# Multiplying the second table's rows by the second layer's weights in layer 1 instead of layer 2 (graph convolution and experts kernel)

## The chip, the cores and the metric

The kernel runs on one core of a Trainium2 chip. The metric is the device time of one execution in microseconds (us), the median over several executions. A difference of 0.2% is about what the measurement of this kernel can tell from none.

## What is computed

There are N = 12500 nodes with D = 256 features and E = 200000 weighted edges. The input is layer-normalised, goes through two graph convolutions, is added to the input, layer-normalised again and sent through a mixture of 8 experts of which each row uses 2.

```python
def _gcn_conv(x, src, dst, ew, W, b, n_nodes):
    xW = x @ W
    deg = segment_sum(ew, dst) + 1.0
    dinv = rsqrt(deg)
    norm = dinv[src] * ew * dinv[dst]
    agg = segment_sum(norm[:, None] * xW[src], dst)
    agg = agg + (dinv * dinv)[:, None] * xW
    return agg + b

h1 = relu(_gcn_conv(layernorm(x), ..., W1, b1))
h2 = relu(_gcn_conv(h1, ..., W2, b2))
x = x + h2
t = layernorm(x)
out = x + t + sum_e combine[:, e] * (gelu(t @ w1[e] + b1[e]) @ w2[e] + b2[e])
```

Everything is float32. The sum over edges is linear, so the product with a layer's weights can be taken before the sum or after it.

## The kernel before

**Setup (to about 234 us).** Edges are sorted by destination. They are cut into 392 groups of 512 edges (4 tiles of 128). Degrees and statistics are worked out, and a first table `ytab[0]` is stored in HBM: normalised rows of x times `dinv`, 98 blocks of 128 nodes. The same rows, transposed, start the accumulator `accbuf` (features on partitions, nodes along the free axis).

**A layer.** GpSimd (POOL) walks through the 392 groups, and for each it issues four indirect DMAs (L480) that gather 128 rows each of the table into `msg`, a ring of MR = 5 groups. Before it writes a ring place again it waits for `s_part`, the count of groups that TensorE has finished. VectorE builds for each tile a one-hot selection times the edge weight (`selection`, L1105). TensorE multiplies (`products`, L811): 8 matmuls per group, a [feature, node] sum over a window of 96 nodes. VectorE adds it into `accbuf` (`add`, L1113). In layer 1 the first group of each pair waits for the messages of both groups.

**A slot.** After every 4 groups one block of 128 nodes is finished; there are 98 such slots in a layer.

In layer 1 a slot is: ScalarE copies the block's sums to `aggS` (`sums`, L562); TensorE multiplies them by the weights (`sums`, L747: two matmuls of 128x256 into `psG`); VectorE scales and adds the bias (`linear`, L1162), then takes the maximum with 0 and scales by `dinv` (`table2`, L1169) into `yS`, which is the row block of the second table; SyncE stores it to `ytab[1]` (L400); TensorE transposes it (`turn_y2`, L755, two transposes) and ScalarE copies the result back into `accbuf` (`back`, L567) as the start of layer 2's sums. Layer 2's gathers may begin only when all 98 blocks are stored (`s_y2out`).

In layer 2 the slot starts alike (`sums` with `gw[1]`, L747, then `linear`), adds the input row, normalises (`moments`, `newton`, `token`), transposes the token (`turn_tok`, L764), computes the router's logits (L772) and the combine weights, and runs the 8 experts: `hidden` (L796), Gelu on ScalarE (L593), `project` (L805) and `share` on VectorE (L1233). Every engine's order is written out by hand. TensorE spreads the experts of the slot before (`last`) between the four groups of the current slot; `sums(1, s)` stands between `hidden(last, 2)` and `project(last, 1)`.

A float32 matmul is two records in the trace, a transpose is one; so `sums` shows as x4, `turn_y2` as x2 and a group of `products` as x16.

Of the kernel before, what the change touches and what calls it, by code (L numbers as in the profile page):

```python
# [8 lines left out]
ALU = mybir.AluOpType  # L9
# [11 lines left out]
R = 4  # L21
# [33 lines left out]
def build(nc, x, src, dst, ew, gw1, gb1, gw2, gb2, rw, ew1, eb1, ew2, eb2, out):  # L55
# [123 lines left out]
    yS = xS  # L179
    res = [sb(f"res{u}", [P, D]) for u in range(2)]  # L180
# [32 lines left out]
    ps_lin, ps_b2 = psG[:, 0:D], psG[:, D:2 * D]  # L213
    ps_tok, ps_lg, ps_comb = psT[:, 0:D], psT[:, D:D + NEXP], psT[0:NEXP, 384:512]
# [69 lines left out]
    s_linD = [sem(f"s_linD{l}") for l in range(2)]  # L284
    s_y2 = sem("s_y2")
# [208 lines left out]
    def _(act):  # L494
# [62 lines left out]
        def sums(l, s):  # L557
            wait(act, s_lin[l], s.k - 1)
            if l == 0:
                wait(act, s_y2C, s.k - 1)  # L560
            stand(act, s)
            act.activation(aggS[:, :, :], accT[:, :, bass.ds(s.col, P)], ACT.Copy).then_inc(s_agg[l], 1)  # L562

        def back(s):
            act.wait_ge(s_y2T, s.k)
            stand(act, s)
            act.activation(accT[:, :, bass.ds(s.col, P)], ps_tok.rearrange("p (k n) -> p k n", k=KD), ACT.Copy).then_inc(s_y2C, 1)  # L567
# [28 lines left out]
        def late0(s):  # L596
            sums(0, s)
            back(s)
# [10 lines left out]
        for k in range(1, NI + 1):  # L609
            s = Slot(k, k % 2, col=slot_word(act, C1, k))  # L610
            act.wait_ge(s_added, k * R)
            sums(0, s)
            back(s)
# [28 lines left out]
    def _(pe):  # L642
# [97 lines left out]
        def sums(l, s, biases_behind=1):  # L740
            pe.wait_ge(s_agg[l], s.k)
            wait(pe, s_linD[l], s.k - 1)
            if l == 1:
# [4 lines left out]
            m.then_inc(s_lin[l], 1)  # L748

        def turn_y2(s):  # L750
            pe.wait_ge(s_y2, s.k)
            wait(pe, s_y2C, s.k - 1)
            stand(pe, s)
            for k in range(KD):
                t = pe.transpose(psT[:, k * P:(k + 1) * P], yS[s.u][:, k * P:(k + 1) * P], ident[:, :])  # L755
            t.then_inc(s_y2T, 1)
# [83 lines left out]
        def late0(s):  # L840
            sums(0, s)
            turn_y2(s)
# [13 lines left out]
        for i in range(NI):  # L856
            s = Slot(i, i % 2) if i else None
            group(0, R * i)
            group(0, R * i + 1)
# [6 lines left out]
        sums(0, Slot(NI, NI % 2))  # L866
        turn_y2(Slot(NI, NI % 2))
# [56 lines left out]
    def _(v):  # L924
# [317 lines left out]
        def late0(s):  # L1242
            linear(0, s)
            table2(s)
# [20 lines left out]
        v.wait_ge(s_spare, 16)  # L1265
# [3 lines left out]
        for i in range(NI):  # L1269
            s = Slot(i, i % 2, entry=slot_word(v, E1, i)) if i else None  # L1270
            bases = bases_at(v, NI - 1 - i)
            for r in range(R):
                q = i * R + r
                add(q, bases[R - 1 - r])
                if q + R < NG:
                    selection(q + R)
                if s and r == 1:
                    linear(0, s)
                    table2(s)
        s = Slot(NI, NI % 2, entry=slot_word(v, E1, NI))  # L1280
        linear(0, s)
        table2(s)
# [88 lines left out]
```

## Time and profile before

| what | value |
|---|---|
| median of 3 runs | 4566.18 us (4564.49 to 4569.79) |
| the profiled execution | 4561.83 us |
| its span | 4560.0 us |
| TensorE busy over the span | 82% |
| GpSimd busy over the span | 67% |
| VectorE, ScalarE busy | 49%, 16% |
| setup, layer 1, layer 2 | to 234 us, to 2212 us, to the end |
| granted TensorE clock, 1000 to 2000 us | 0.75 |
| granted TensorE clock, 2400 to 3400 us | 1.00 |

The profile is one execution; its time is 4.35 us (0.1%) under the median. "Busy" is the union of the instructions of an engine, and TensorE's weight loads are counted apart (PEld). A line of the timeline gives start, length, engine, line and operation, how many records it merges, and in brackets the idle time ahead of it and what ended that. As matmuls overlap, the cost of a run of matmuls in a dense stretch is the distance from its start to the start of the next run, which is shorter than its own length. The granted clock of 1.00 is 2.4 GHz, 0.50 is 1.2 GHz.

### The profile page before, as it was taken

Reading aid. Unit: us, or ns where it says so; the run is one execution under the profiler, and the core shown is the slowest. Engines: PE = TensorE matmul, PEld = TensorE weight load, DVE = VectorE, ACT = ScalarE, POOL = GpSimd, SP = SyncE. Lnnn points to the kernel's source line nnn. Section 1 sums busy time; section 2 is a strip of 40 time slices with the busy share of each in tenths; the row PEclk is TensorE's granted clock in tenths of the full one; section 3 lists DMA queues with packets and bytes.
Section 4 is the critical chain, followed back from the end, with each engine's and each line's share of the span. In section 5 each row is a group of like instructions: output and inputs, shape, how many; then the busy total and the mean of one; then the engine's idle time right before and its main releaser. Section 6 shows DMA issues by size and latency. Waiting matters only on the chain.

```text
span 4560.0 us, 77688 instructions
## 1 busy us (share of the span) xinstructions
PE 3746.5 (82%) x27282; PEld 3519.0 (77%) x27283; DVE 2222.0 (49%) x8238; ACT 725.4 (16%) x2287; POOL 3035.8 (67%) x3196
## 2 busy tenths in 40 slices
PE   6756666666666666666699999999999999999999
PEld 5556565656656655665699999999999999999999
DVE  7623232332333323223366666666666666666665
ACT  1300000000000000000022222222222222222222
POOL 2177777777777777777676666666666666666663
PEclk9967777777777777777799999999999999999999
DMA  6443333333333333333333333333333333333331
GB/s 144 120 135 111 112 112 112 111 112 112 111 112 112 111 112 112 111 112 112 100 112 101 104 101 99 101 102 102 103 101 99 101 102 102 103 100 100 101 102 56
DMA packets 242001, 488.03 MB, mean 107 GB/s; under 512 B 59886, under 2 KB 140089, under 8 KB 241612
## 3 DMA queue, kind: packets, MB, share of 16 engines
q0 software_dynamic: 150528, 411.24, 31.9%
q1 hardware_dynamic: 84424, 66.74, 4.8%
q10 hardware_dynamic: 6660, 5.02, 0.4%
q8 instruction: 225, 3.69, 0.3%
q14 instruction: 164, 1.34, 0.1%
HBM read 444.10 MB, written 38.67 MB: 106 GB/s over the span
## 4 chain that ended last, share of the span: by engine, by line
PE 54%; POOL 31%; issue 11%; DMA 3%; DVE 0%; ACT 0%; SPq 0%; ACTq 0%; DVEq 0%; POOLq 0%
POOL msg L480 31%; PE part L811 16%; PE psY L805 16%; PE psH L796 15%; PE psG L747 2%; DMA msg<-ytab,srcT 1%; PE psG L787 1%; PE psT L772 1%; PE psY L687 1%; DMA ytab<-msg 1%; PE psH L811 1%; PE psT L764 0%; POOL sel L452 0%; PE psY L811 0%; PE psG L687 0%
## 5 line engine op out<-in xcount | busy, mean ns | idle before, releaser
L480 POOL DMA_INDIRECT msg<-ytab,srcT x3136 | 2987.9, 953 | 1362.4 <-issue 893.1
L811 PE MATMUL part<-sel,msg 128*128 128x96 f32 x8384 | 1147.7, 299 | 270.8 <-DMA msg<-ytab,srcT 270.8
L811 PEld LDWEIGHTS part<-sel,msg 128*128 128x128 f32 x8384 | 1121.8, 216 | 297.9 <-DMA msg<-ytab,srcT 254.4
L796 PEld LDWEIGHTS psH<-work,wbuf 128*128 128x128 f32 x6272 | 808.7, 192 | 34.8
L805 PE MATMUL psY<-wbuf,work 128*128 128x256 f32 x3136 | 829.6, 387 | 0.0
L1105 DVE TENSOR_SCALAR sel<-iota,relT,ewT 128x96 f32<-128x96 f32 x3136 | 826.4, 341 | 2.3 <-ACT accbuf L553 1.4
L796 PE MATMUL psH<-work,wbuf 128*128 128x128 f32 x6272 | 811.1, 275 | 0.0
L593 ACT ACTIVATE work<-psH,b_s 128x128 f32<-128x128 f32 x1568 | 489.7, 363 | 1586.1 <-PE psH L796 1586.1
L1113 DVE TENSOR_TENSOR accbuf<-accbuf,part 128x192 f32 x524 | 185.7, 354 | 1076.7 <-PE part L811 1076.6
L805 PEld LDWEIGHTS psY<-wbuf,work 128*128 128x128 f32 x3136 | 543.7, 191 | 77.5 <-issue 32.5
L811 PE MATMUL psY<-sel,msg 128*128 128x96 f32 x2080 | 388.6, 374 | 236.6 <-DMA msg<-ytab,srcT 236.6
L811 PEld LDWEIGHTS psY<-sel,msg 128*128 128x128 f32 x2080 | 377.6, 286 | 257.2 <-DMA msg<-ytab,srcT 257.2
L811 PE MATMUL psH<-sel,msg 128*128 128x96 f32 x2080 | 379.1, 368 | 235.4 <-DMA msg<-ytab,srcT 235.4
L811 PEld LDWEIGHTS psH<-sel,msg 128*128 128x128 f32 x2080 | 368.4, 279 | 256.0 <-DMA msg<-ytab,srcT 256.0
L1233 DVE SCALAR_TENSOR_TENSOR work<-psY,comb,work 128x256 f32<-128x256 f32 x686 | 329.3, 480 | 56.4 <-PE psY L805 35.2
L567 ACT ACTIVATE accbuf<-psT 128x256 f32 x98 | 37.5, 383 | 1849.2 <-PE psT L755 1849.2
L1113 DVE TENSOR_TENSOR accbuf<-accbuf,psY 128x192 f32 x130 | 46.1, 355 | 463.6 <-PE psY L811 463.6
L1113 DVE TENSOR_TENSOR accbuf<-accbuf,psH 128x192 f32 x130 | 46.1, 355 | 451.8 <-PE psH L811 451.8
L747 PE MATMUL psG<-gw,work 128*128 128x256 f32 x784 | 205.4, 385 | 1.1 <-ACT work L562 1.1
L1162 DVE SCALAR_TENSOR_TENSOR work<-psG,dinv,gb 128x256 f32<-128x256 f32 x196 | 94.2, 480 | 103.4 <-PE psG L747 103.4
L747 PEld LDWEIGHTS psG<-gw,work 128*128 128x128 f32 x784 | 135.2, 193 | 11.4 <-ACT work L562 1.3
L452 POOL TENSOR_TENSOR sel<-sel,ewT 128x192 f32<-128x192 f32 x49 | 44.1, 899 | 101.2 <-DVE sel L966 95.8
(184 smaller groups left out, 1768.8 us busy)
## 6 DMA issues: line engine op xcount, KB each, us to landing
msg<-ytab,srcT POOLq DMA_INDIRECT x3136
ytab<-xS SPq DMA_DIRECT2D x99, 128.0 KB, 1.9
ytab<-msg SPq DMA_DIRECT2D x98, 128.0 KB, 1.9
xS<-in_x SPq DMA_DIRECT2D x98, 128.0 KB
out<-res SPq DMA_DIRECT2D x98, 128.0 KB
accbuf<-in_x SPq DMA_DIRECT2D x97, 128.0 KB, 3.2
wbuf<-in_L_ffn_w ACTq DMA_DIRECT2D x2, 2048.0 KB, 14.8
wbuf<-in_dst SPq DMA_DIRECT2D x1, 588.0 KB
```

The source lines that it names most:

```text
L480: pool.indirect_dma_start(msg[:, r * GT + j, :], None, ytab[l], bass.IndirectOffsetOnAxis(ap=srcT[:, g * GT + j:g * GT + j + 1].bitcast(U3 ...
L593: g = act.activation(hS[:, e % 2, m, :], psH[e % 2][:, m * P:(m + 1) * P], ACT.Gelu, bias=b1_s[:, e, m:m + 1])
L687: m = pe.matmul(wbanks[t // SB][0:LO, at_col:at_col + HI], wlo[:, h, r * GT + k, :], whi[:, h, r * GT + k, :], start=(k == 0), stop=(k == ...
L747: m = pe.matmul(ps_lin, aggS[:, k, :], gw[l][:, k, :], start=(k == 0), stop=(k == KD - 1))
L772: m = pe.matmul(ps_lg, tokS[s.u][:, k, :], rwT[:, k, :], start=(k == 0), stop=(k == KD - 1))
L796: mm = pe.matmul(psH[e % 2][:, m * P:(m + 1) * P], w1_s[:, e, k, m * P:(m + 1) * P], tokS[s.u][:, k, :], start=(k == 0), stop=(k == KD - 1))
L805: mm = pe.matmul(psY[e % 2][:, 0:D], hS[:, e % 2, m, :], w2_s[:, e, m, :], start=(m == 0), stop=(m == KD - 1))
L811: m = pe.matmul(slot[:, h * W:(h + 1) * W], msg[:, tile0 + j, h * P:(h + 1) * P], sel[:, sel0 + j, :], start=(j == 0), stop=(j == GT - 1))
L1105: t = v.tensor_scalar(sel[:, r * GT + j, :], iota[:, 0:W], relT[:, g * GT + j:g * GT + j + 1], ewT[:, g * GT + j:g * GT + j + 1], ALU.is_e ...
L1113: v.tensor_tensor(to, to, sums_of(q // NG, q % NG)[:, 0:KD * W].rearrange("p (k w) -> p k w", k=KD), ALU.add).then_inc(s_added, 1)
L1162: v.scalar_tensor_tensor(lin[:, :], ps_lin, dinv[:, bass.ds(s.entry, 1)], gb[l][:, :], ALU.mult, ALU.add).then_inc(s_linD[l], 1)
L1233: v.scalar_tensor_tensor((mix if e < NEXP - 1 else res[s.u])[:, :], psY[e % 2][:, 0:D], comb[s.u][:, e:e + 1], (mix if e else front[s.u])[ ...
```

## The change

In layer 1, VectorE now writes the hidden rows to `h1` (a buffer that layer 2 uses for `tok`), not to `yS`. TensorE transposes them (`turn_h1`), ScalarE copies them to `h1T`, TensorE multiplies them by `gw[1]` (`table2`, two matmuls of 128x256 into the second half of `psG`), and ScalarE copies the product to `yS`. From there the store, the two transposes and the copy back go as before, but half a slot to a slot later. In layer 2, `sums` no longer multiplies by `gw[1]`: it turns the sums by two transposes into the same place.

```diff
@@ ScalarE
+        def hidden1(s):
+            act.wait_ge(s_h1T, s.k)
+            wait(act, s_tab, s.k - 1)
+            act.activation(h1T[:, :, :], ps_h1.rearrange("p (k n) -> p k n", k=KD), ACT.Copy).then_inc(s_h1C, 1)
+        def table2(s):
+            act.wait_ge(s_tab, s.k)
+            wait(act, s_y2out, (s.k - 2) * 16)
+            wait(act, s_y2T, s.k - 2)
+            act.activation(yS[s.u][:, :], ps_tab, ACT.Copy).then_inc(s_y2, 1)
-        def back(s):
+        def back(s, taken):
             act.wait_ge(s_y2T, s.k)
+            act.wait_ge(s_agg[0], taken)
...
-        for k in range(1, NI + 1):
-            s = Slot(k, k % 2, col=slot_word(act, C1, k))
-            act.wait_ge(s_added, k * R)
-            sums(0, s)
-            back(s)
+        for k in range(1, NI + 2):
+            last, s = s, Slot(k, k % 2, col=slot_word(act, C1, k)) if k <= NI else None
+            if last:
+                hidden1(last)
+                table2(last)
+            if s:
+                act.wait_ge(s_added, k * R)
+                sums(0, s)
+            if last:
+                back(last, min(k, NI))
@@ TensorE
             for k in range(KD):
-                m = pe.matmul(ps_lin, aggS[:, k, :], gw[l][:, k, :], start=(k == 0), stop=(k == KD - 1))
+                if l == 0:
+                    m = pe.matmul(ps_lin, aggS[:, k, :], gw[0][:, k, :], start=(k == 0), stop=(k == KD - 1))
+                else:
+                    m = pe.transpose(ps_lin[:, k * P:(k + 1) * P], aggS[:, k, :], ident[:, :])
+        def turn_h1(s):
+            pe.wait_ge(s_h1, s.k)
+            wait(pe, s_y2C, s.k - 1)
+            for k in range(KD):
+                t = pe.transpose(ps_h1[:, k * P:(k + 1) * P], h1[:, k * P:(k + 1) * P], ident[:, :])
+            t.then_inc(s_h1T, 1)
+        def table2(s):
+            pe.wait_ge(s_h1C, s.k)
+            pe.wait_ge(s_linD[0], s.k)
+            for k in range(KD):
+                m = pe.matmul(ps_tab, h1T[:, k, :], gw[1][:, k, :], start=(k == 0), stop=(k == KD - 1))
+            m.then_inc(s_tab, 1)
...
             if s:
                 sums(0, s)
-            group(0, R * i + 2)
-            group(0, R * i + 3)
-            if s:
-                turn_y2(s)
+            if last:
+                turn_y2(last)
+            if i < NI:
+                group(0, R * i + 2)
+                group(0, R * i + 3)
+            if s:
+                turn_h1(s)
+                table2(s)
@@ VectorE
-        def table2(s):
+        def hidden1(s):
             v.wait_ge(s_linD[0], s.k)
-            wait(v, s_y2out, (s.k - 2) * 16)
-            wait(v, s_y2T, s.k - 2)
+            wait(v, s_h1T, s.k - 1)
-            v.tensor_scalar(yS[s.u][:, :], lin[:, :], 0.0, dinv[:, bass.ds(s.entry, 1)], ALU.max, ALU.mult).then_inc(s_y2, 1)
+            v.tensor_scalar(h1[:, :], lin[:, :], 0.0, dinv[:, bass.ds(s.entry, 1)], ALU.max, ALU.mult).then_inc(s_h1, 1)
...
-        v.wait_ge(s_spare, 16)
```

The wait on `s_spare` (the store of the padding rows) moves from VectorE to ScalarE.

TensorE's order over one slot in the middle of layer 1, before: two groups, the sums' product, two groups, the transposes of the table's block.

```order
L811 MATMUL part<-sel,msg 128x96 [waits s_sel,s_msg3]
L811 MATMUL part<-sel,msg 128x96 x7
L747 MATMUL psG<-gw,work 128x256 [waits s_linD0,s_agg0]
L747 MATMUL psG<-gw,work 128x256
L811 MATMUL psH<-sel,msg 128x96 [waits s_sel,s_msg4,s_msg0]
...
L811 MATMUL psH<-sel,msg 128x96 x7
L755 MATMUL psT<-ident,xS 128x128 [waits s_y2C,s_y2]
L755 MATMUL psT<-ident,xS 128x128
L811 MATMUL psY<-sel,msg 128x96 [waits s_sel,s_msg1,s_msg2]
```

The same place after the change. L864 is `products`, L781 the sums' product, L808 the transposes of the table's block (now of the slot before), L792 the transposes of the hidden rows, L800 the product with `gw[1]`.

```order
L864 MATMUL part<-sel,msg 128x96 [waits s_sel,s_msg3]
L864 MATMUL part<-sel,msg 128x96 x7
L781 MATMUL psG<-gw,work 128x256 [waits s_y2,s_linD0,s_agg0]
L781 MATMUL psG<-gw,work 128x256
L808 MATMUL psT<-ident,xS 128x128 [waits s_y2C,s_y2]
L808 MATMUL psT<-ident,xS 128x128
L864 MATMUL psH<-sel,msg 128x96 [waits s_sel,s_msg4,s_msg0]
...
L864 MATMUL psH<-sel,msg 128x96 x7
L792 MATMUL psT<-ident,work 128x128 [waits s_y2C,s_h1]
L792 MATMUL psT<-ident,work 128x128
L800 MATMUL psG<-gw,work 128x256 [waits s_linD0,s_h1C]
L800 MATMUL psG<-gw,work 128x256
```

The table's transposes moved from behind the second pair to behind the sums' product, one slot later; behind the second pair stand two transposes and two matmuls with a wait for ScalarE (`s_h1C`) between them.

TensorE's order in layer 2 around `sums(1, s)`, before and then after (L805 and L858 are `project`, L796 and L849 `hidden`):

```order
L796 MATMUL psH<-work,wbuf 128x128 [waits s_gelu]
L796 MATMUL psH<-work,wbuf 128x128 x3
L747 MATMUL psG<-gw,work 128x256 [waits s_bias,s_linD1,s_agg1]
L747 MATMUL psG<-gw,work 128x256
L805 MATMUL psY<-wbuf,work 128x256 [waits s_yadd,s_gelu]
```

```order
L849 MATMUL psH<-work,wbuf 128x128 [waits s_gelu]
L849 MATMUL psH<-work,wbuf 128x128 x3
L784 MATMUL psG<-ident,work 128x128 [waits s_bias,s_linD1,s_agg1]
L784 MATMUL psG<-ident,work 128x128
L858 MATMUL psY<-wbuf,work 128x256 [waits s_yadd,s_gelu]
```

Two transposes of 128 columns stand where two matmuls of 256 columns stood, with the same waits.

## Rows read from the trace of the kernel before

**Rows 1.** The page, busy time of each engine over the span.
```profile
PE 3746.5 (82%) x27282; PEld 3519.0 (77%) x27283; DVE 2222.0 (49%) x8238; ACT 725.4 (16%) x2287; POOL 3035.8 (67%) x3196
```

**Rows 2.** Windows: stretch, length, busy us of each engine, PEclk, DMA share, GB/s.
```profile
1000.00:2000.00 1000.00, 640.27 (x3486) 605.78 (x3485) 303.14 (x1099) 39.96 (x100) 756.85 (x799) 0.75 0.39 112
2400.00:3400.00 1000.00, 1000.00 (x7332) 943.40 (x7331) 636.15 (x2458) 256.81 (x850) 650.30 (x680) 1.00 0.36 102
```

**Rows 3.** Groups by form, 600 to 2100 us (layer 1): GpSimd's gathers.
```profile
L480 POOL DMA_INDIRECT msg<-ytab,srcT x1198 | 1135.8, 948 | 364.8 <-issue 359.1 <-PE part L811 2.4 <-PE psH L811 1.8
```

**Rows 4.** Timeline of one slot of layer 1, TensorE.
```profile
1502.15 0.38 PE L755 MATMUL psT<-ident,xS 128*128 128x128 f32 x2
...
1508.55 6.54 PE L811 MATMUL part<-sel,msg 128*128 128x96 f32 x32 [6.02 <-DMA msg<-ytab,srcT]
...
1514.93 1.06 PE L747 MATMUL psG<-gw,work 128*128 128x256 f32 x4
...
1518.48 3.81 PE L811 MATMUL psH<-sel,msg 128*128 128x96 f32 x32 [2.49 <-DMA msg<-ytab,srcT]
```

**Rows 5.** Timeline of TensorE in layer 2: transposes, sums, and the last slot's sums.
```profile
3407.17 0.38 PE L764 MATMUL psT<-ident,work 128*128 128x128 f32 x2
3407.39 1.92 PE L811 MATMUL part<-sel,msg 128*128 128x96 f32 x16
...
3420.30 1.03 PE L747 MATMUL psG<-gw,work 128*128 128x256 f32 x4
3421.17 1.03 PE L805 MATMUL psY<-wbuf,work 128*128 128x256 f32 x4
...
4528.02 1.03 PE L747 MATMUL psG<-gw,work 128*128 128x256 f32 x4
```

**Rows 6.** Timeline of the other engines in the same slot of layer 2.
```profile
3420.50 0.62 ACT L593 ACTIVATE work<-psH,b_s 128x128 f32<-128x128 f32 x2 [1.49 <-PE psH L796]
...
3421.47 0.48 DVE L1162 SCALAR_TENSOR_TENSOR work<-psG,dinv,gb 128x256 f32<-128x256 f32 x1 [1.02 <-PE psG L747]
...
3426.87 0.94 POOL L480 DMA_INDIRECT msg<-ytab,srcT  x1 [2.39 <-PE part L811]
...
3430.10 0.41 DVE L1194 TENSOR_SCALAR work<-work,mv,rs 128x256 f32<-128x256 f32 x1
...
3430.66 0.25 PEld L764 LDWEIGHTS psT<-ident,work 128*128 128x128 f32 x2
```

**Rows 7.** Timeline, from layer 1's last group to layer 2's first gather.
```profile
2205.33 0.38 PE L755 MATMUL psT<-ident,xS 128*128 128x128 f32 x2
...
2205.75 0.38 ACT L567 ACTIVATE accbuf<-psT 128x256 f32 x1 [19.30 <-PE psT L755]
2206.32 0.42 ACT L562 ACTIVATE work<-accbuf 128x256 f32 x1 [0.19 <-ACT accbuf L567]
...
2206.79 1.13 PE L747 MATMUL psG<-gw,work 128*128 128x256 f32 x4 [1.08 <-ACT work L562]
2208.06 0.48 DVE L1162 SCALAR_TENSOR_TENSOR work<-psG,dinv,gb 128x256 f32<-128x256 f32 x1 [2.08 <-PE psG L747]
2208.58 0.35 DVE L1169 TENSOR_SCALAR xS<-work,dinv 128x256 f32<-128x256 f32 x1
...
2209.10 0.33 SPq L400 DMA_DIRECT2D ytab<-xS  x1
...
2211.91 0.94 POOL L480 DMA_INDIRECT msg<-ytab,srcT  x1 [13.96 <-DMA ytab<-xS]
```

**Rows 8.** Windows and timeline, start of layer 2, at the lower clock level.
```profile
2212.00:2225.00 13.00, 3.81 (x18) 3.84 (x19) 1.41 (x6) 0.00 (x0) 9.96 (x11) 0.50 0.60 114
...
2221.19 6.88 PE L811 MATMUL part<-sel,msg 128*128 128x96 f32 x32 [11.77 <-DMA msg<-ytab,srcT]
...
2241.89 1.97 PE L747 MATMUL psG<-gw,work 128*128 128x256 f32 x4
...
2243.65 2.46 PE L811 MATMUL part<-sel,msg 128*128 128x96 f32 x16
```

More of the change, by code:

```diff
@@ L179, in build @@
     yS = xS
+    h1, h1T = tok, tokS[0]
     res = [sb(f"res{u}", [P, D]) for u in range(2)]
@@ L284, in build @@
     s_linD = [sem(f"s_linD{l}") for l in range(2)]
+    s_h1 = sem("s_h1")
+    s_h1T = sem("s_h1T")
+    s_h1C = sem("s_h1C")
+    s_tab = sem("s_tab")
     s_y2 = sem("s_y2")
@@ L559, in sums @@
             if l == 0:
-                wait(act, s_y2C, s.k - 1)
+                wait(act, s_y2C, s.k - 2)
             stand(act, s)
             act.activation(aggS[:, :, :], accT[:, :, bass.ds(s.col, P)], ACT.Copy).then_inc(s_agg[l], 1)
-        def back(s):
+        def hidden1(s):
+            act.wait_ge(s_h1T, s.k)
+            wait(act, s_tab, s.k - 1)
+            stand(act, s)
+            act.activation(h1T[:, :, :], ps_h1.rearrange("p (k n) -> p k n", k=KD), ACT.Copy).then_inc(s_h1C, 1)
[3 more added lines that the diff above has]
+            wait(act, s_y2T, s.k - 2)
+            stand(act, s)
+            act.activation(yS[s.u][:, :], ps_tab, ACT.Copy).then_inc(s_y2, 1)
+        def back(s, taken):
             act.wait_ge(s_y2T, s.k)
+            act.wait_ge(s_agg[0], taken)
             stand(act, s)
-            act.activation(accT[:, :, bass.ds(s.col, P)], ps_tok.rearrange("p (k n) -> p k n", k=KD), ACT.Copy).then_inc(s_y2C, 1)
+            act.activation(accT[:, :, bass.ds(s.col, P)], ps_y2.rearrange("p (k n) -> p k n", k=KD), ACT.Copy).then_inc(s_y2C, 1)
         def token(s):
@@ L597, in late0 @@
             sums(0, s)
-            back(s)
+            hidden1(s)
+            table2(s)
+            back(s, s.k)
         def late1(s):
@@ L608, in _ @@
         act.wait_ge(s_tables, 1)
-        for k in range(1, NI + 1):
-            s = Slot(k, k % 2, col=slot_word(act, C1, k))
-            act.wait_ge(s_added, k * R)
-            sums(0, s)
-            back(s)
+        act.wait_ge(s_spare, 16)
+        s = None
+        for k in range(1, NI + 2):
[8 more added lines that the diff above has]
+                back(last, min(k, NI))
         with act.If(general(act) > 0):
@@ L742, in sums @@
             wait(pe, s_linD[l], s.k - 1)
-            if l == 1:
+            if l == 0:
+                wait(pe, s_y2, s.k - 1)
+            else:
                 wait(pe, s_bias, s.k - biases_behind)
@@ L754, in turn_y2 @@
             for k in range(KD):
-                t = pe.transpose(psT[:, k * P:(k + 1) * P], yS[s.u][:, k * P:(k + 1) * P], ident[:, :])
+                t = pe.transpose(ps_y2[:, k * P:(k + 1) * P], yS[s.u][:, k * P:(k + 1) * P], ident[:, :])
             t.then_inc(s_y2T, 1)
@@ L841, in late0 @@
             sums(0, s)
+            turn_h1(s)
+            table2(s)
             turn_y2(s)
@@ L854, in late1 @@
             project(s, NEXP - 1)
[L856 to L859, printed above, removed]
+        s = None
+        for i in range(NI + 1):
+            last, s = s, Slot(i, i % 2) if i else None
+            if i < NI:
+                group(0, R * i)
+                group(0, R * i + 1)
             if s:
                 sums(0, s)
-            group(0, R * i + 2)
-            group(0, R * i + 3)
+            if last:
+                turn_y2(last)
+            if i < NI:
+                group(0, R * i + 2)
+                group(0, R * i + 3)
             if s:
-                turn_y2(s)
-        sums(0, Slot(NI, NI % 2))
-        turn_y2(Slot(NI, NI % 2))
+                turn_h1(s)
+                table2(s)
+        turn_y2(s)
         with pe.If(general(pe) > 0):
@@ L1243, in late0 @@
             linear(0, s)
-            table2(s)
+            hidden1(s)
         def late1(s):
@@ L1278, in _ @@
                     linear(0, s)
-                    table2(s)
+                    hidden1(s)
         s = Slot(NI, NI % 2, entry=slot_word(v, E1, NI))
         linear(0, s)
-        table2(s)
+        hidden1(s)
         with v.If(general(v) > 0):
```

5 lines of the change are left out of this document (added).

## The prediction

> **What bounds the kernel now.** The page comes first: no engine is busy all the time, TensorE is the busiest at 82% [rows 1]. Such a share is a mean over stages, so the windows come next. They show two different kernels. In layer 1 TensorE is busy 640 of 1000 us at a granted clock of 0.75; in layer 2 it is busy 1000 of 1000 us at 1.00, its upper level of 2.4 GHz [rows 2]. GpSimd is busy 757 us in the first and 650 us in the second.
>
> Then the groups, to see what GpSimd's idle time is. In layer 1 its 1198 gathers take 1135.8 us and leave 364.8 us idle, 359.1 us of that "issue", that is nobody's fault but its own; all waits for TensorE together are under 6 us [rows 3]. So a gather costs (1135.8 + 364.8) / 1198 = 1.253 us, a slot of 16 gathers 20.0 us, and layer 1 is bound by GpSimd. In one slot of it the timeline shows TensorE idle 6.02 us ahead of one pair of groups and 2.49 us ahead of the other, both times for a gather [rows 4].
>
> In layer 2 the distance from the first slot's sums to the last one's is 4528.02 - 2241.89 = 2286.1 us for 97 slots, 23.57 us each [rows 5, 8]. That is more than the 20.0 us of 16 gathers, and GpSimd waits for TensorE there (2.39 us in the one row shown) [rows 6]. Layer 2 is bound by TensorE's instruction stream. What leaves that stream in layer 2 is time gained; what enters it in layer 1 falls into idle time, as long as it fits.
>
> **Layer 2, the part removed.** `sums` costs TensorE the distance from its start to the next run: 3421.17 - 3420.30 = 0.87 us for four records [rows 5]. The two transposes that replace it have the shape and type of the token's transposes, which cost 3407.39 - 3407.17 = 0.22 us [rows 5]. I take that row as it is; the operands differ only in the buffer. The gain is 0.65 us a slot, and 98 slots give **-63.7 us**. Bounds for the unseen cost of the transposes in this place: 0.22 us (no better row exists) and, if they were no faster per record than the product's records (0.87 / 4 = 0.22 us each), 0.44 us, which would leave 0.43 us a slot or 42 us.
>
> On the price per column the Trainium skill has a figure ("TensorE: Matmul & The Clock Gate", section Terms, the entry xbus): a transpose mode that is 4x faster for FP32. The row bears out half of that: 0.11 us for 128 columns against 0.22 us for a record of 256, of which a matmul has two, so a transpose is 2x faster per column than the product. By the page's figure two transposes would cost an estimated 0.11 us and the gain would be 74 us.
>
> Does the gain stay? Three links leave from that place. (1) Gelu of `hidden(last, 2)` starts at 3420.50 and ends at 3421.12; the next product that needs it is `project(last, 2)`, two runs and 1.75 us behind `project(last, 1)`, so at 3422.9; 0.65 us less still leaves over 1 us [rows 5, 6]. (2) VectorE waited 1.02 us for `sums` ahead of `linear`, so it is ready earlier too and everything behind it keeps its distance to TensorE [rows 6]. (3) The tightest link is the token: VectorE ends it at 3430.51 and TensorE's weight load for its transposes starts at 3430.66, with no idle time marked [rows 6]. But both sides of it lie behind `sums` and move together. GpSimd keeps 22.9 - 20.0 = 2.9 us a slot. The first slot is different: TensorE is at the lower level there, `sums` takes 1.76 us [rows 8], and VectorE has a one-hot build in front of `linear`; I count it as any other slot.
>
> **Layer 1, the part added.** Each slot gets two transposes (0.22 us) and two matmuls (0.87 us) more on TensorE, with a wait for a copy by ScalarE between them. The copy is like L567, 0.38 us, and comes 0.42 us after the transposes start [rows 7]; so the block behind the second pair takes some 0.42 + 0.38 + 0.1 + 1.1 = 2.0 us. Before, two transposes stood there and then 6.02 us of idle time [rows 4]; 4 us of it are left. The moved transposes of the table's block go behind the sums' product, where 2.49 us were idle; 2.3 us are left. Their `s_y2` is a whole pair old by then. So no group starts later, `s_part` comes as before, and GpSimd's 20.0 us a slot stay. VectorE's instruction has the same shape; ScalarE, 4% busy here [rows 2], gets two copies more; the store is the same DMA, later. The wait for `s_spare` was met long before on either engine. Cost: **0**. If the cover were gone, the price is the full 2.0 us a slot.
>
> **Between the layers.** Here nothing covers. Layer 2's first gather waits for the last store, and the chain is in [rows 7]. Two things lengthen it. First, ScalarE must finish slot 97's two copies before slot 98's sums: transposes at 2205.3, copy to 2206.13, product to about 2207.4, copy to 2207.8, so the sums start at 2207.95, not 2206.32: +1.65 us. Second, slot 98's own hidden rows go through transposes (to the copy's start 0.47 us), copy 0.38, product with its hops 1.35, copy 0.4 and the store's issue: in place of the 0.17 us from VectorE's end to the store, about 2.8 us. Sum **+4.3 us**. At the lower clock level three products would each be 0.9 us longer, which makes 7 us the upper end; 3 us is the lower.
>
> **The sum.** -63.7 + 0 + 4.3 = -59.4 us. Against the profiled execution 4561.8 - 59.4 = 4502.4 us; that execution is 4.35 us under the median of the runs, so against the median 4566.2 - 59.4 = **4506.8 us**, 1.3% less.
>
> **Rivals.**
>
> *A. The gain turns into waits.* TensorE arrives earlier and waits for the token or for Gelu. For it: link (3) has 0.15 us to spare. Against: no idle time at the product's place, VectorE idles 1.02 us ahead of `linear`. If all of it came back, the time is 4566.2 + 4.3 = 4570.5 us; if half, 4539 us.
>
> *B. Layer 1 becomes TensorE's (slower).* The granted clock is 0.75 there, so part of it runs at the lower level, and it could stay there throughout. Then a slot costs two pairs at 6.88, the sums' product 1.76 and the new one 1.76 [rows 8], four transposes 0.88 (twice the 0.22) and the hop to ScalarE about 0.85: 19.0 us against GpSimd's 20.0. It decides from 20.0 us a slot, and the whole kernel is slower from 20.6, which eats the 59.4 us. With 2 us more of waits a slot it would be 21.0, and the time 4506.8 + 98 = 4605 us. Against it: 1.0 us is left even at the lower level, a ring of five groups stands between the engines, and more work on TensorE has no reason to lower its clock.
>
> *C. Transposes pull TensorE's clock down in layer 2 (slower).* If the clock fell behind the new transposes for no more than one group, that group of 16 records would cost as much as one in the lower level, 6.88 / 2 = 3.4 us in place of about 1.75, and 98 slots give +162 us: 4669 us. Against: the token's two transposes stand in front of a group in every slot now, that group takes 1.92 us, and the window's granted clock is 1.00 [rows 2, 5]. The Trainium skill ("TensorE: Matmul & The Clock Gate", Part 4: PE-mode transpose) says that a transpose does not count as busy for the clock gate as a matmul does; the trace agrees only in so far as it does not speak against it, since 0.22 us among 23 us of products leave nothing to see.
>
> *D. The change doesn't do what it says.* The order of TensorE's instructions shows the 128-column transposes in place of the product, so this has no chance of its own.
>
> **Chances.** Forecast 0.90, A 0.06 (half of it partial, half full), B 0.02, C 0.02. Within the forecast the unknowns are the boundary (3 to 7 us), the spread of the median (the three runs span 5.3 us, 0.1%) and the price of the transposes; by that and a share of A the range is 4500 to 4519 us. What measurement can tell from no change is 0.2%, 9 us: the forecast and the partial A lie beyond it (0.93 faster), full A within it (0.03), B and C above (0.04).
>
> **What would show each step.** In the changed profile: TensorE still 1000 of 1000 us in layer 2 at clock 1.00, about 22.9 us from one slot's sums to the next, and 0.22 us from the start of L784 to the next run; no idle time ahead of the token's transposes. In layer 1 a gather every 1.253 us, waits of GpSimd for TensorE still some us in total, TensorE busy about 70%. First gather of layer 2 near 2216 us. The prediction is wrong if GpSimd waits for TensorE in layer 1, if the slot of layer 2 stays above 23.2 us, or if the granted clock of layer 2 is under 1.00.

## The result and the profile after

The changed kernel takes 4507.74 us (median of 4 runs, 4506.43 to 4508.78), the kernel before beside it 4565.34 us (median of 4). The ratio is 0.9873, 95% interval [0.9856, 0.989]: 57.6 us less. Forecast were 4506.8 us and 59.4 us less.

The profiled execution takes 4507.62 us, its span 4505.8 us. The span can be cut at the same four instructions in each trace: GpSimd's first gather of layer 1, its last, VectorE's last add of layer 1, GpSimd's first gather of layer 2.

| stretch, us | before | after | difference |
|---|---|---|---|
| setup, to the first gather | 233.9 | 237.9 | +4.0 |
| layer 1, first gather to last | 1963.1 | 1966.3 | +3.2 |
| last gather to last add | 8.6 | 6.8 | -1.9 |
| last add to layer 2's first gather | 6.28 | 9.25 | +2.97 |
| layer 2 | 2348.1 | 2285.6 | -62.5 |

Only the last two rows are put down to the change. The twelve executions that were profiled later start their gathers between 233 and 239 us, whichever kernel it is, and gathers of layer 1 by the changed route take 1963.6 and 1963.3 us in e5 and e7 below. The last gather to the last add goes with the clock level that the last pair of groups meets: its run takes 5.44 us before, 3.81 us here, and 5.44 us again in e7, where the stretch is 8.3 us.

The windows after (stretch, length, busy us of each engine, PEclk, DMA share, GB/s) answer to [rows 2]:

```profile
1000.00:2000.00 1000.00, 666.49 (x3780) 612.79 (x3780) 302.81 (x1092) 72.83 (x200) 757.10 (x798) 0.81 0.39 112
...
2400.00:3400.00 1000.00, 1000.00 (x7453) 945.76 (x7452) 653.36 (x2529) 264.42 (x873) 663.54 (x699) 1.00 0.37 104
```

Layer 1 moves the same 112 GB/s with the same 757 us of GpSimd, and TensorE's busy time is up by 26 us only, although 1.09 us more in each of 50 slots makes 54 us: its granted clock rose from 0.75 to 0.81 with more to do. Layer 2 is still full of TensorE at 1.00. GpSimd's gathers in layer 1 (the groups view, 600 to 2100 us) answer to [rows 3]; a gather costs (1136.0 + 364.5) / 1196 = 1.255 us, and the waits for TensorE are some 3 us in all:

```profile
L487 POOL DMA_INDIRECT msg<-ytab,srcT x1196 | 1136.0, 950 | 364.5 <-issue 361.2 <-PE part L864 1.2 <-PE psY L864 1.2
```

One slot of layer 1 on TensorE, in order of time, answers to [rows 4]. The added block (L792, then the wait of 0.47 us for ScalarE, then L800) ends at 1512.63, and TensorE still sits idle for 1.80 us until a gather lands. Over the 75 slots from 600 to 2100 us it is 3.40 us in the mean there, and 2.75 us ahead of the other pair. Behind L781 stand the moved transposes:

```profile
1510.64 0.38 PE L792 MATMUL psT<-ident,work 128*128 128x128 f32 x2
...
1511.50 1.13 PE L800 MATMUL psG<-gw,work 128*128 128x256 f32 x4 [0.47 <-ACT work L575]
...
1514.43 3.81 PE L864 MATMUL part<-sel,msg 128*128 128x96 f32 x32 [1.80 <-DMA msg<-ytab,srcT]
...
1518.08 1.06 PE L781 MATMUL psG<-gw,work 128*128 128x256 f32 x4
...
1518.97 0.38 PE L808 MATMUL psT<-ident,xS 128*128 128x128 f32 x2
```

The place of the removed product in layer 2 answers to [rows 5, 6]. The transposes' start to the next run is 3420.50 - 3420.29 = 0.21 us (0.218 us in all 87 slots from 2400 to 4400 us where no record is missing), and VectorE's wait ahead of `linear` went from 1.02 to 0.39 us, so it is no later relative to TensorE:

```profile
3420.29 0.38 PE L784 MATMUL psG<-ident,work 128*128 128x128 f32 x2
...
3420.50 1.03 PE L858 MATMUL psY<-wbuf,work 128*128 128x256 f32 x4
3420.81 0.48 DVE L1222 SCALAR_TENSOR_TENSOR work<-psG,dinv,gb 128x256 f32<-128x256 f32 x1 [0.39 <-PE psG L784]
```

Between the layers (timeline; answers to [rows 7]):

```profile
2210.96 0.35 DVE L1173 TENSOR_TENSOR accbuf<-accbuf,part 128x192 f32 x1 [1.43 <-PE part L864]
...
2212.96 0.41 ACT L569 ACTIVATE work<-accbuf 128x256 f32 x1
...
2215.21 0.35 DVE L1228 TENSOR_SCALAR work<-work,dinv 128x256 f32<-128x256 f32 x1
...
2217.70 0.38 ACT L582 ACTIVATE xS<-psG 128x256 f32<-128x256 f32 x1 [1.22 <-PE psG L800]
...
2218.25 0.33 SPq L407 DMA_DIRECT2D ytab<-xS  x1
...
2220.21 0.95 POOL L487 DMA_INDIRECT msg<-ytab,srcT  x1 [15.07 <-DMA ytab<-xS]
```

### The profile page after: what moved, and what is told of

The parts are those of the page before. It is cut to its first block, busy times and chain, and to the rows that moved or that the text cites. A ratio compares the mean times of both kernels' runs of the same rounds, so it can differ in the third digit from the quotient of the medians.

```text
span 4505.8 us, 79156 instructions
## 1 busy us (share of the span) xinstructions
PE 3743.4 (83%) x27674; PEld 3487.0 (77%) x27675; DVE 2224.4 (49%) x8238; ACT 791.8 (18%) x2483; POOL 3028.2 (67%) x3196
## 3 DMA queue, kind: packets, MB, share of 16 engines
q0 software_dynamic: 150528, 411.24, 32.4%
## 4 chain that ended last, share of the span: by engine, by line
PE 53%; POOL 32%; issue 12%; DMA 2%; DVE 0%; ACT 0%; SPq 0%; ACTq 0%; DVEq 0%; POOLq 0%
POOL msg L487 32%; PE psY L858 16%; PE part L864 16%; PE psH L849 16%; PE psG L840 1%; DMA msg<-ytab,srcT 1%; DMA ytab<-msg 1%; PE psT L825 1%; PE psY L718 1%; PE psT L817 0%; PE psG L784 0%; POOL sel L459 0%; PE psY L864 0%; PE psH L864 0%; PE psG L718 0%
## 5 line engine op out<-in xcount | busy, mean ns | idle before, releaser
L864 PE MATMUL part<-sel,msg 128*128 128x96 f32 x8384 | 1126.4, 295 | 238.4 <-DMA msg<-ytab,srcT 238.4
L864 PEld LDWEIGHTS part<-sel,msg 128*128 128x128 f32 x8384 | 1100.0, 212 | 265.6 <-DMA msg<-ytab,srcT 222.5
L849 PEld LDWEIGHTS psH<-work,wbuf 128*128 128x128 f32 x6272 | 808.8, 192 | 35.4
L858 PE MATMUL psY<-wbuf,work 128*128 128x256 f32 x3136 | 829.4, 387 | 0.0
L849 PE MATMUL psH<-work,wbuf 128*128 128x128 f32 x6272 | 811.5, 275 | 0.0
L858 PEld LDWEIGHTS psY<-wbuf,work 128*128 128x128 f32 x3136 | 535.1, 191 | 73.2 <-issue 32.5
L864 PE MATMUL psY<-sel,msg 128*128 128x96 f32 x2080 | 361.0, 355 | 201.5 <-DMA msg<-ytab,srcT 201.5
L864 PE MATMUL psH<-sel,msg 128*128 128x96 f32 x2080 | 355.0, 351 | 202.7 <-DMA msg<-ytab,srcT 202.7
L864 PEld LDWEIGHTS psY<-sel,msg 128*128 128x128 f32 x2080 | 350.1, 267 | 222.1 <-DMA msg<-ytab,srcT 222.1
L864 PEld LDWEIGHTS psH<-sel,msg 128*128 128x128 f32 x2080 | 344.0, 263 | 223.3 <-DMA msg<-ytab,srcT 223.3
L575 ACT ACTIVATE work<-psT 128x256 f32<-128x256 f32 x98 | 37.6, 384 | 735.1 <-PE psT L792 735.1
L800 PE MATMUL psG<-gw,work 128*128 128x256 f32 x392 | 110.8, 405 | 46.4 <-ACT work L575 46.4
L800 PEld LDWEIGHTS psG<-gw,work 128*128 128x128 f32 x392 | 66.4, 189 | 74.7 <-ACT work L575 69.6
```

What stands on the lines that cost most here:

```text
L800: m = pe.matmul(ps_tab, h1T[:, k, :], gw[1][:, k, :], start=(k == 0), stop=(k == KD - 1))
L849: mm = pe.matmul(psH[e % 2][:, m * P:(m + 1) * P], w1_s[:, e, k, m * P:(m + 1) * P], tokS[s.u][:, k, :], start=(k == 0), stop=(k == KD - 1))
L858: mm = pe.matmul(psY[e % 2][:, 0:D], hS[:, e % 2, m, :], w2_s[:, e, m, :], start=(m == 0), stop=(m == KD - 1))
L864: m = pe.matmul(slot[:, h * W:(h + 1) * W], msg[:, tile0 + j, h * P:(h + 1) * P], sel[:, sel0 + j, :], start=(j == 0), stop=(j == GT - 1))
```

## The experiments

**Two kinds of chip.** The runs went to several chips. On the ones that e5, e6, e7 and e12 had, the kernel before takes about 4563 us, as in the prediction. On the two that e1 to e4 and e8 to e11 had, it takes 4990.7 and 4991.4 us. The times of the second kind are compared with the kernel before on the same chip alone.

What differs there shows in the timeline of layer 1, here of e8. TensorE's matmuls come one by one, mostly 0.7 us or a multiple of it apart, with the idle time marked "issue", for some 10 us in each slot. And what waits for TensorE is released long after TensorE's record has ended: the sums' product (L748) ends at 1499.58, VectorE's operation on it starts at 1509.02; the transposes (L758) end at 1510.64, ScalarE's copy of them starts at 1516.27, and GpSimd goes on at 1516.30.

```profile
1498.52 1.06 PE L748 MATMUL psG<-gw,work 128*128 128x256 f32 x4
...
1509.02 0.48 DVE L1165 SCALAR_TENSOR_TENSOR work<-psG,dinv,gb 128x256 f32<-128x256 f32 x1 [3.48 <-remote]
1509.95 0.69 PE L758 MATMUL psT<-ident,xS 128*128 128x128 f32 x2 [0.51 <-issue]
...
1511.75 0.32 PE L814 MATMUL psY<-sel,msg 128*128 128x96 f32 x1 [1.11 <-issue]
1513.86 0.32 PE L814 MATMUL psY<-sel,msg 128*128 128x96 f32 x1 [1.79 <-issue]
1515.26 0.32 PE L814 MATMUL psY<-sel,msg 128*128 128x96 f32 x1 [1.08 <-issue]
...
1516.27 0.38 ACT L567 ACTIVATE accbuf<-psT 128x256 f32 x1 [21.02 <-remote]
1516.30 0.94 POOL L480 DMA_INDIRECT msg<-ytab,srcT  x1 [3.30 <-remote]
```

From 1000 to 2000 us TensorE's semaphore events come a median 4.5 us behind the end of the record that sends them (e8; 4.7 in e1, 1.9 to 2.7 in the traces with the changed layer 1); in every trace of the first kind it is 0.01 us, and for VectorE and ScalarE in e8 it is 0.01 us as well. "Remote" is what the profile writes where it finds no record that ended just before the event. So either TensorE's work ends late or its signals do, and its records alone do not say when it worked. "TensorE comes late" below means this, and its cause stays open. Two rivals can be looked up: the gathers' queue has 150528 packets with a mean of 0.155 us each in e8 as in the changed kernel on the first kind, and the queues that bring instructions have 224 and 178 packets in e8 and in e12, with means of 1.13 and 0.42 us against 1.07 and 0.41. That is 6% at most on 224 packets, which leaves the 9% of the whole time unexplained.

**e1, e8, e12: layer 2's part alone.** The kernel before, with this edit; the product with the second weights is left out.

```diff
-                m = pe.matmul(ps_lin, aggS[:, k, :], gw[l][:, k, :], start=(k == 0), stop=(k == KD - 1))
+                if l == 0:
+                    m = pe.matmul(ps_lin, aggS[:, k, :], gw[0][:, k, :], start=(k == 0), stop=(k == KD - 1))
+                else:
+                    m = pe.transpose(ps_lin[:, k * P:(k + 1) * P], aggS[:, k, :], ident[:, :])
```

> The kernel before, with only layer 2's sums turned by two transposes instead of multiplied by the second weights; the product is left out of the computation altogether. Theory 1 (TensorE's stream in layer 2 is the whole gain): 0.87 - 0.22 = 0.65 us less in each of 98 slots, -64 us against before, about 4501 to 4503 us, layer 1 and the stretch between the layers as before (first gather of layer 2 about 6.3 us behind the last add of layer 1). Rival (the gain of the whole change comes in part from layer 1 or from the table's changed route): less than 60 us gained here.

> The same kernel as e1_l2_only, which ran on a chip where the kernel before took 4990.7 us and layer 1 moved 98 GB/s in place of 112; layer 2 was no longer full of TensorE there. Asked again, on a chip like the first if it comes to that: with the kernel before near 4565 us, theory 1 still says -64 us, the rival less than 60 us of gain. If this chip is like that of e1 (kernel before near 4990 us), about -41 us again.

> The kernel of e1 and e8 a third time, as the last run, for a chip on which the kernel before takes about 4565 us (e5 to e7 had one). Theory 1: -64 us against before, about 4501 us, a slot of layer 2 at 22.96 us as in the changed kernel, layer 1 and the stretch between the layers as before. Rival (part of the change's gain comes from layer 1): less than 60 us of gain. If the kernel before takes about 4990 us again: -37 to -41 us, and the question stays as e1 and e8 leave it.

On the first kind of chip (e12): 4499.17 us against 4563.32, ratio 0.9861 [0.9844, 0.9877], **64.2 us less**; expected 64. Its layer 2 takes 2285.5 us, the changed kernel's 2285.6; its last add to first gather is 6.28 us, and layer 1's gathers 1963.2 us, as before. The whole gain is made in layer 2, and the rival that layer 1 adds to it falls. On the second kind: 4949.7 against 4990.7 (e1) and 4954.0 against 4991.4 (e8), 41 and 37 us less; TensorE is busy 890 of 1000 us from 2400 to 3400 us there (e1), so its stream does not fill all of layer 2.

**e2, e9: layer 1's part alone.** The changed kernel, with the product kept in layer 2 too, so that it is taken twice.

```diff
-                    m = pe.transpose(ps_lin[:, k * P:(k + 1) * P], aggS[:, k, :], ident[:, :])
+                    m = pe.matmul(ps_lin, aggS[:, k, :], gw[1][:, k, :], start=(k == 0), stop=(k == KD - 1))
```

> The changed kernel, with layer 2's sums multiplied by the second weights as before, so that this product is taken twice. Theory 1: the added work of layer 1 is hidden, only the chain between the layers grows by about 3 us as in the changed kernel's trace (9.25 us from last add to first gather against 6.28): +2 to +5 us against before, 4568 to 4571 us; a slot of layer 2 is 23.6 us again. Rival (layer 1 pays for the added work, and layer 2 gains more than 64 us to cover it): more than +8 us against before, and GpSimd waiting for TensorE in layer 1.

> The same kernel as e2_l1_only. With the kernel before near 4565 us theory 1 still says +2 to +5 us, the rival over +8 us. If the chip is like that of e2, about +22 us again.

Both ran on the second kind: 5012.4 against 4990.7 (ratio 1.004 [1.0026, 1.0055]) and 5017.5 against 4991.4 (1.0058 [1.0041, 1.0075]), 22 and 26 us more. There the added work is **not** hidden. Layer 1's gathers take 2264.4 and 2260.9 us against 2244.0 and 2247.3 in e1 and e8, 17 us more, and the last gather to the last add takes 13.3 and 14.7 us against 9.6 and 6.8, 6 us more. But layer 1 was not GpSimd's alone there to begin with. In e8, whose layer 1 is that of the kernel before, GpSimd waits 210.1 us "remote" from 600 to 2100 us, once a slot and for up to 3.3 us each time, and every one of these waits ends with an event of `s_part`, TensorE's count; waits longer than 0.4 us make 211 us in e8 and 232 us in e9. The groups view of layer 1 in e8 and then in e9, and in e9's timeline a transpose pair (L792) whose record ends at 1515.91 and whose copy by ScalarE starts at 1526.73, so that TensorE waits 11.26 us for it:

```profile
L480 POOL DMA_INDIRECT msg<-ytab,srcT x1046 | 991.1, 947 | 509.4 <-issue 291.5 <-remote 210.1 <-PE part L814 2.7
```

```profile
L487 POOL DMA_INDIRECT msg<-ytab,srcT x1037 | 981.4, 946 | 519.7 <-issue 288.9 <-remote 78.4 <-PE psY L864 52.1
```

```profile
1515.53 0.38 PE L792 MATMUL psT<-ident,work 128*128 128x128 f32 x2
1527.17 2.07 PE L800 MATMUL psG<-gw,work 128*128 128x256 f32 x4 [11.26 <-ACT work L575]
```

This is what rival B describes (TensorE's turn comes too late for the ring), for another reason than the clock, and with the ring late already before the added work. For the first kind of chip the part's cost comes by difference: the changed kernel gained 57.6 us and e12 64.2, so layer 1's part costs about 6.5 us, with 3.0 us of it seen between the layers and the rest within what two medians can differ by. The changed kernel itself did not run on the second kind; if the two parts add up there, +22 to +26 and -37 to -41 would leave it some 11 to 19 us under the kernel before (an estimate).

**e3, e10: a product with the identity in place of the transpose.**

```diff
-                    m = pe.transpose(ps_lin[:, k * P:(k + 1) * P], aggS[:, k, :], ident[:, :])
+                    m = pe.matmul(ps_lin[:, k * P:(k + 1) * P], aggS[:, k, :], ident[:, :], start=True, stop=True)
```

> The changed kernel, with each of the two transposes of layer 2's sums as a plain matmul with the identity (128 columns). Theory 1 (what counts is the distance between records in TensorE's stream, 0.11 us for one record of 128 columns; a float32 matmul has two records, a transpose one): 0.44 us in place of 0.22, +0.22 us in each of 98 slots, +21.6 us against the changed kernel, about 4529 us, and still 42 us under before. Rival (a transpose is 4 times faster per column than a float32 matmul, so its 0.22 us would be held up by something else): a matmul's record of 128 columns costs 0.11 us elsewhere in this trace, so a price over 0.5 us a slot would be needed to see it. Rival (the slot is held by another chain, and TensorE's stream has room): no change against the changed kernel.

> The same kernel as e3_identity_product. With the kernel before near 4565 us theory 1 says +21.6 us against the changed kernel, that is -36 us against before (near 4529 us); the rival that the slot is held by another chain says -57 us.

Both on the second kind: 5012.6 and 5010.6 us. In stretches without gaps the row gives the price (e10, timeline of TensorE): 3417.87 - 3417.42 = 0.45 us for four records, against 0.218 for the transposes' two. In 73 slots of layer 2 the median is 0.447 us.

```profile
3417.42 0.61 PE L784 MATMUL psG<-ident,work 128*128 128x128 f32 x4
3417.87 1.03 PE L858 MATMUL psY<-wbuf,work 128*128 128x256 f32 x4
```

So a record of 128 columns costs 0.11 us, be it a transpose or half of a float32 matmul, and the transpose wins by having one record. This is the 2x per column of the prediction, not the 4x that the Trainium skill gives for FP32 ("TensorE: Matmul & The Clock Gate", Terms), without saying against what; with 4x against the float32 product the transposes' run would be an estimated 0.11 us. The effect on the whole time of the first kind of chip (+21.6 us) was not measured. On the second kind layer 2 takes 2447 and 2455 us with two transposes (e1, e8), 2487 and 2488 with four records of 128 columns (e3, e10), and 2492 and 2489 with four of 256 (e2, e9): halving the columns gives 1 to 5 us, taking out two records 32 to 42. So where TensorE comes late the number of its instructions seems to count and not their length. This is argued, not shown: e1 and e8 differ from the others in layer 1's route too.

**e4, e11: where layer 2's next bound lies.** Half of the first expert product is left out.

```diff
-                for k in range(KD):
-                    mm = pe.matmul(psH[e % 2][:, m * P:(m + 1) * P], w1_s[...], tokS[s.u][:, k, :], start=(k == 0), stop=(k == KD - 1))
+                for k in range(1):
+                    mm = pe.matmul(psH[e % 2][:, m * P:(m + 1) * P], w1_s[...], tokS[s.u][:, k, :], start=True, stop=True)
```

> The changed kernel, with half of the first expert product left out (only the first 128 of 256 input features), to see where TensorE stops to bound layer 2. It takes 4 of 8 records, 0.44 us, from each of 8 experts: 3.5 us a slot, from 22.96 to 19.4 us. Theory 1: GpSimd's 16 gathers take over at 20.0 to 20.1 us a slot, so about 2.9 us a slot are gained, -284 us, near 4224 us, GpSimd's waits for TensorE nearly gone in layer 2. Rival (TensorE, VectorE and ScalarE form a chain near the present slot): a slot stays above 21 us, 4320 us or more.

> The same kernel as e4_floor, which was slower than the kernel before where it ran, at a granted clock of 0.85 to 0.90 in layer 2. With the kernel before near 4565 us theory 1 still says a slot of 20.0 to 20.1 us and 4224 us. The rival, formed on e4: once TensorE has to wait for gathers its clock falls to the lower level for parts of the slot, and the chain of products and copies at that level takes longer than the gathers: a slot over 21 us with a granted clock under 0.95, 4320 us or more.

5239.2 and 5234.3 us, ratios 1.0509 [1.0484, 1.0534] and 1.0487 [1.0469, 1.0504]: a kernel with 3.5 us a slot less to multiply is **slower** than the kernel before, by 249 and 243 us. Both runs were on the second kind. Layer 2 takes 2700.9 us, 27.6 a slot. From 3400 to 4400 us TensorE stops for up to 5.4 us at a time marked issue, and GpSimd waits for it for 243 us, where theory 1 has these waits nearly gone (e4):

```profile
3400.00:4400.00 1000.00, 813.09 (x5107) 739.47 (x5105) 553.04 (x2130) 221.22 (x735) 558.33 (x588) 0.90 0.31 88
```

```profile
3415.93 1.62 PE L858 MATMUL psY<-wbuf,work 128*128 128x256 f32 x4 [4.68 <-issue]
```

The clock is at 0.90 there, as the rival formed on e4 has it. But the longest stops are marked issue and not a wait for a gather, so the rival's number came and its reason is not shown; on this kind of chip theory 1 is wrong, and for the first kind the floor stays open.

**e5, e6: how much cover layer 1 has.** The changed kernel, with the new product repeated 4 and 12 more times a slot.

```diff
-            for k in range(KD):
+            for k in list(range(KD)) * 5:
                 m = pe.matmul(ps_tab, h1T[:, k, :], gw[1][:, k, :], start=(k == 0), stop=(k == KD - 1))
```

> The changed kernel, with layer 1's new product repeated 4 more times in each slot (the same result written again), 8 matmuls, 16 records, 3.5 us at the upper clock level and 7.0 us at the lower. It measures how much cover the added work has. Theory 1 (GpSimd bounds layer 1 with some 6 us to spare, and more work on TensorE raises its granted clock rather than lowering it): within 2 us of the changed kernel except for the last slot, whose repeated product lies open between the layers, twice (slots 97 and 98), +7 us, about 4515 us; GpSimd's waits for TensorE still under 10 us; granted clock in layer 1 over 0.81. Rival (layer 1 was near its edge, as at the lower clock level, where a slot had 1 us left): several us a slot, up to +300 us.

> The same with 12 more repeats, 48 records, 10.4 us a slot at the upper clock level. TensorE's work in a slot of layer 1 at the upper level is 4 groups x 1.76 + 2 x 0.87 + 2 x 0.22 = 9.2 us, with the wait for ScalarE about 9.8 us; with 10.4 more it is 20.2 us against 20.05 for the gathers. Theory 1 with the clock rising: just at the edge, 0 to 1 us a slot lost, 4530 to 4630 us with 20 us open between the layers; granted clock in layer 1 near 1.00. Rival (the clock stays near 0.81): 23 us or more a slot, over 4800 us.

On the first kind. e5: 4511.92 us (ratio to before 0.9887 [0.987, 0.9903]), 4.2 us over the changed kernel's 4507.74; expected were about 4515. Gathers of layer 1 take 1963.6 us, so all 98 x 3.5 us are free there, although TensorE is no longer idle ahead of one of the two pairs (0.00 us in 75 slots) and 3.83 us in the mean ahead of the other, and last add to first gather grows from 9.25 to 16.17 us, which is the repeated product twice. e6: 4558.36 us (0.9987 [0.9977, 0.9997]), 50.6 us over the changed kernel: gathers 1992.6 us, 29 more than in e5, and 29.98 us between the layers, 21 more than in the changed kernel. The windows (e5, then e6) and a slot of e6 with no idle time for a gather left:

```profile
1000.00:2000.00 1000.00, 782.91 (x4588) 724.92 (x4587) 305.62 (x1100) 72.72 (x200) 756.95 (x799) 0.84 0.39 112
```

```profile
1000.00:2000.00 1000.00, 976.81 (x6083) 891.73 (x6082) 301.94 (x1079) 71.27 (x196) 742.17 (x785) 1.00 0.38 110
```

```profile
1499.98 3.71 PE L864 MATMUL psY<-sel,msg 128*128 128x96 f32 x32
...
1509.04 11.49 PE L800 MATMUL psG<-gw,work 128*128 128x256 f32 x52 [0.47 <-ACT work L575]
1520.37 3.71 PE L864 MATMUL psH<-sel,msg 128*128 128x96 f32 x32
```

e6 sits just behind the edge: 20.39 us a slot in this row against 20.0 of gathers. TensorE had room for over 3.5 and under 10.4 us more a slot. The granted clock went 0.81, 0.84, 1.00 as work was added, and the work beside it became cheaper: a pair of groups whose run takes 6.54 us in [rows 4] takes 3.71 us in every row of e6 here. Rival B of the prediction, at the lower level throughout, falls on this kind of chip.

**e7: the next thing in the way.** The changed kernel, with the second biases' product on 128 rows in place of 8; the added rows are zero.

```diff
-    b2_s = sb("b2_s", [NEXP, D])
+    b2_s = sb("b2_s", [P, D])
-    combT = sb("combT", [NEXP, P])
+    combT = sb("combT", [P, P])
...
-        act.dma_start(b2_s[:, :], eb2).then_inc(s_wts, 16)
+        act.dma_start(b2_s[0:NEXP, :], eb2).then_inc(s_wts, 16)
...
-            act.activation(combT[:, :], ps_comb, ACT.Copy).then_inc(s_combC, 1)
+            act.activation(combT[0:NEXP, :], ps_comb, ACT.Copy).then_inc(s_combC, 1)
...
+        v.memset(b2_s[:, :], 0.0)
+        v.memset(combT[:, :], 0.0)
         v.memset(xS[0][:, :], 0.0).then_inc(s_pads, 1)
```

> The changed kernel, with the product that adds the experts' second biases (8 rows of the array) widened to 128 rows with zeros, to see whether a version beats both. In the trace the run of that product costs 0.62 us for two records that cost 0.22 us each elsewhere, and the weight load behind it sits idle for 0.33 us, marked issue. Theory a (the narrow operand makes TensorE wait before the next full one): 0.33 us less a slot, -32 us against the changed kernel, about 4475 us. Theory b (the stop belongs to the place, a wait on a semaphore, not to the operand): no change, 4507 us.

4480.04 us (4476.9 to 4481.32), ratio to before 0.9814 [0.9798, 0.9831]: 83.7 us under before where the change has 57.6, so 26 us better than the change (27.7 by the two medians), the fastest kernel of the study. Layer 2 takes 2261.6 us, 23.9 less. In the changed kernel (first fence) the run with 8 rows costs 0.62 us and the weight load behind it idles 0.33; with 128 rows (second fence, e7) the run costs 3411.79 - 3411.32 = 0.47 us:

```profile
3425.87 0.69 PE L840 MATMUL psG<-b_s,combT 8*128 8x256 f32 x2
...
3426.49 0.73 PEld L858 LDWEIGHTS psY<-wbuf,work 128*128 128x128 f32 x4 [0.33 <-issue]
```

```profile
3411.32 0.62 PE L840 MATMUL psG<-b_s,combT 128*128 128x256 f32 x2
...
3411.79 1.03 PE L858 MATMUL psY<-wbuf,work 128*128 128x256 f32 x4
...
3414.26 0.94 POOL L487 DMA_INDIRECT msg<-ytab,srcT  x1 [0.30 <-issue]
...
3414.41 1.05 PE L849 MATMUL psH<-work,wbuf 128*128 128x128 f32 x8
...
3414.68 0.65 DVE L1255 TENSOR_SCALAR work<-work,mv,rs 128x256 f32<-128x256 f32 x1
...
3415.38 0.20 PEld L817 LDWEIGHTS psT<-ident,work 128*128 128x128 f32 x2
3415.38 0.44 PE L817 MATMUL psT<-ident,work 128*128 128x128 f32 x2
...
3415.65 1.92 PE L864 MATMUL part<-sel,msg 128*128 128x96 f32 x16
```

The runs ahead of it and behind it are 0.1 us shorter each as well, 0.36 us a slot in all (medians of 87 and 88 slots), so theory a holds: the edit changes the rows of this product's operands and, with them, two buffers. Why the narrow one costs more was not tried. But 0.24 us arrive in the time. The rest goes at the token: the run of `hidden` ahead of its transposes now costs 3415.38 - 3414.41 = 0.97 us, not 0.89, the transposes 0.27, not 0.22 (in the means of all slots 0.12 us together), and their weight load waits for the token's end at 3415.33. VectorE did not start that operation later; it takes longer. The source view of the token's line (min/median/max in ns), in the changed kernel and in e7:

```profile
L1253 DVE TENSOR_SCALAR work<-work,mv,rs x87: 411/413/534, 2419.3 to 4393.8; 128x256 f32<-128x256 f32 x87
```

```profile
L1255 DVE TENSOR_SCALAR work<-work,mv,rs x88: 411/645/652, 2415.1 to 4391.5; 128x256 f32<-128x256 f32 x88
```

In e7 a gather starts 0.42 us ahead of it (3414.26), in the changed kernel 0.72 us ahead. All fourteen traces, on both kinds of chip, agree on what that does. Where the operation starts up to 0.41 us behind a gather, or 0.68 us and more behind it, it takes some 0.41 us. Where it starts 0.41 to 0.59 us behind, it is longer, and its end always stands 1.06 to 1.07 us behind the gather's start: 194 times, 75 of them in e7 and 4 in the changed kernel. So a faster TensorE moved GpSimd's gathers against VectorE's operation, and one operation on the tightest link pays for where it now falls. The Trainium skill ("GPSIMD Engine Reference", 8. Key points) has GpSimd share its memory interfaces with VectorE and contend with some of VectorE's instructions; the rows agree in kind, though none tells whether this operation is one of those. That the gather sets the length follows from these times; which part of its work does it was not tried, nor was a gather moved to win the 0.12 us back.

## Why the prediction was right

**Layer 2, the part removed: right.** -63.7 us were forecast; the traces show -62.5 and, in e12, -62.6 (-64.2 in the medians). The price of the transposes, taken from the token's row at 0.22 us, is 0.22 in place, and the usual slot went from 23.60 to 22.96 us, 0.65 us less. The missing 1.2 us lie mostly at the start of the layer, which the prediction counted as any other slot: from the first gather to the second slot's sums it takes 52.2 us, not 51.8. The three links kept their distance, as VectorE's wait of 0.39 us and the full 1000 of 1000 us show; the token starts 9.15 us behind the sums' start, 0.65 us sooner than before (9.80).

**Layer 1, the part added: right on this kind of chip.** GpSimd's waits for TensorE did not grow, and e5 shows that even 3.5 us more a slot are free. The estimate of the idle time left (4 and 2.3 us) rests on one slot, and its 6.02 us are near the most that any of 75 slots has ahead of that pair (2.6 to 6.17, mean 4.26). After the change the means are 3.40 and 2.75 us and the least 0.98 and 0.81 us, so the room was there, but less of it in the tightest slots than the prediction says; e5 shows that a pair may even lose all its idle time, as the ring holds. On the second kind of chip this step is wrong: e2 and e9 put 17 us on layer 1's gathers, where GpSimd waits for TensorE without the added work too (e8).

**Between the layers: the mechanism right, the term too large.** +4.3 us were forecast, +2.97 measured, the same 9.25 to 9.27 us in all eight executions of the new route without repeated products. By its steps: the sums start 1.31 us later, not 1.65 (2212.96 - 2210.96 = 2.00 against 0.69 before); VectorE's end to the store is 2.69 us against 0.17, +2.5, as forecast; and the store's start to the first gather is 1.96 us, where before it was 2.81. That last 0.85 us nobody forecast, and what shortens it was not tried. The trace's two differences, -62.5 and +2.97, make -59.5 us against -59.4 forecast: two misses of 1.2 and 1.3 us offset each other, and that the sum fits to 0.1 us is luck.

**The rivals.** A did not come in the change, but e7 shows its mechanism at work a few tenths of a microsecond further on: less work ahead of the token's transposes than the token needs. B is refuted by e5 and e6 for the first kind of chip; for the second its outcome, not its cause, is seen in e2 and e9. C: the granted clock of layer 2 stayed at 1.00.

## What to carry to other kernels

Ask of each stage which engine it waits for, then move work from the stage where that engine is full to one where it idles; the price of what stays behind is the distance between the starts of neighbouring runs in a dense stretch, and a row of the same shape gave it to 0.01 us. Take idle time from many slots and not from one: here the one shown had nearly the most. Behind the first edit the next tight link shows: here a hand-over with 0.15 us to spare, named before the run, that took a third of the following gain (0.36 us saved a slot, 0.24 seen). And cover that is ample on one chip may be used up on another, so a gain that rests on hiding work should be measured on more than one; when an engine's records and the waits for it disagree, as on the second kind of chip, go by the waits.

## What was not expected of the hardware

- Two chips ran the same kernel 9% slower (4990.7 and 4991.4 against about 4563 us). There TensorE's signals come a median 1.9 to 4.7 us behind the end of its records in layer 1 (0.01 us elsewhere), its matmuls stand 0.7 us or a multiple apart in stretches, and DMA packets are as fast as elsewhere. A kernel with less to multiply was 5% slower there.
- A product with 8 rows between ones of 128 costs 0.36 us more than the same with 128 rows, 0.1 us of it on either side.
- The same VectorE operation on 128x256 took 0.41 us, or up to 0.65 us where it started 0.41 to 0.59 us behind a gather of GpSimd; its end then stood 1.06 to 1.07 us behind the gather's start, 194 times out of 194.
- TensorE's granted clock in layer 1 rose with added work: 0.75 before, 0.81 in the changed kernel, 0.84 in e5 and 1.00 in e6.
